# Patch stage of a vision tower: ScalarE writes the normalised rows two units ahead

## The reference

```python
x = features.reshape(B, c, h, 16, w, 16) -> (B, h * w, 16 * 16 * 3)   # 196 patches of 768 numbers an image
x = _layernorm(x, ln1_g, ln1_b)                                       # over the 768
x = jnp.einsum('bnd,de->bne', x, W) + b                               # to 192 features
x = _layernorm(x, ln2_g, ln2_b)                                       # over the 192
h = x                                                                 # the tokens; attention and the rest follow
```

## Time and profile before

| | us |
|---|---|
| time of the kernel, median of three runs | 3089.83 (3086.55 to 3103.68) |
| the profiled execution: its own time | 3087.19 |
| the profiled execution: span of the instructions | 3085.5 |
| patch stage in it: first `xn` to last `yn` | 31.6 to 368.0 |
| busy over the whole span: PE, PEld, DVE, ACT, POOL | 2732.0, 2124.6, 2311.9, 1878.1, 1682.0 |

### The profile page before, as it was taken

The page is one execution under the profiler, slowest core; times in us unless marked ns, Lnnn a source line. Parts: engine busy times, 40 slices in busy tenths (PEclk is TensorE's granted clock), DMA queues, the critical chain, the costliest instruction groups (busy, mean ns, idle before and its releaser), DMA issues. The chain is left out here.

```text
span 3085.5 us, 95504 instructions
## 1 busy us (share of the span) xinstructions
PE 2732.0 (89%) x31491; PEld 2124.6 (69%) x31491; DVE 2311.9 (75%) x5326; ACT 1878.1 (61%) x3798; POOL 1682.0 (55%) x1957
## 2 busy tenths in 40 slices
PE   5798788999899998989998967999986999999998
PEld 5688645555555555555555546899975888888887
DVE  5689678788878887877788735877765777777776
ACT  5577556667666666666666636777753444444443
POOL 3467635555455666667666432567674444444444
PEclk9899989999999999999999968999987999999999
DMA  6555256676766667676767635444433444444443
GB/s 159 161 157 166 58 121 155 145 164 149 157 142 152 165 163 167 161 173 160 175 159 174 143 76 136 147 147 147 143 126 91 68 67 65 68 67 65 69 66 47
DMA packets 515433, 395.07 MB, mean 128 GB/s; under 512 B 223136, under 2 KB 488386, under 8 KB 515138
## 3 DMA queue, kind: packets, MB, share of 16 engines
q1 hardware_dynamic: 431426, 310.47, 41.3%
q0 software_dynamic: 38496, 46.38, 8.5%
q10 hardware_dynamic: 45216, 34.34, 4.6%
HBM read 232.59 MB, written 155.42 MB: 126 GB/s over the span
## 5 line engine op out<-in xcount | busy, mean ns | idle before, releaser
L814 DVE TENSOR_REDUCE a_mx<-a_mxp 98x4 f32<-98x784 f32 x768 | 747.0, 973 | 268.6 <-PE a_mxp L1000 265.9
L603 ACT ACTIVATE a_pt<-a_st 98x784 f32<-98x784 f32 x768 | 634.6, 826 | 352.8 <-PE a_st L986 351.9
L1817 POOL DMA_INDIRECT out_dram<-f_yo,f_idg x202 | 330.9, 1638 | 415.6 <-DVE f_yo L2158 378.9
L500 POOL TENSOR_TENSOR a_cf<-a_ctxs,a_rec 128x1176 f32<-128x1176 f32 x64 | 171.6, 2681 | 448.1 <-DMA a_rec<-a_recip 448.1
L1895 ACT ACTIVATE f_hf<-f_bank,f_b1c 128x256 f32<-128x256 f32 x606 | 254.3, 473 | 236.0 <-PE f_bank L1128 236.0
L1015 PE MATMUL a_pv<-a_pt,a_vp 98*32 98x196 f32 x6144 | 358.7, 352 | 5.0 <-issue 4.1
L986 PE MATMUL a_st<-a_qst,a_kst 49*128 49x196 f16 x3072 | 266.7, 253 | 78.6 <-DMA a_qst<-a_mrow 53.5
L2320 PE MATMUL f_bank<-f_w2h,f_hh 128*128 x1212 | 298.9, 247 | 19.0 <-DVE f_hl L2142 18.7
L2321 PE MATMUL f_bank<-f_w2h,f_hl 128*128 x1212 | 298.2, 246 | 0.0
L2322 PE MATMUL f_bank<-f_w2l,f_hh 128*128 x1212 | 298.2, 246 | 0.0
L1000 PE MATMUL a_mxp<-a_kst,a_qst 48*128 48x196 f16 x3072 | 263.6, 250 | 28.8 <-DVE a_mx L814 21.5
(11 more groups left out here) (314 smaller groups left out, 8269.9 us busy)
## 6 DMA issues: line engine op xcount, KB each, us to landing
a_rec<-a_recip SPq DMA_DIRECT2D x256, 147.0 KB, 4.9
t_rows<-in_x_dram SPq DMA_DIRECT2D x84, 392.0 KB, 5.7
a_qst<-a_qk SPq DMA_DIRECT2D x256, 110.2 KB, 3.2
a_kst<-a_qk SPq DMA_DIRECT2D x256, 110.2 KB, 4.0
f_xg<-f_listed SPq DMA_DIRECT2D x101, 264.0 KB, 2.8
a_qk<-a_qkh SPq DMA_DIRECT2D x128, 196.0 KB, 3.1
a_qk<-a_qkl SPq DMA_DIRECT2D x128, 98.0 KB, 3.4
a_qk<-a_qkh SPq DMA_DIRECT2D x128, 98.0 KB, 2.5
```

What stands on the lines that cost most here:

```text
L603: act.activation(pt[k % PT][:].rearrange("p j a t -> p j (a t)"), st_ps[0:half_t, :, 0:unit_t], ACT.Exp, scale=sm_scale).then_inc(exp_s, 1)
L814: dve.tensor_reduce(mx[:, a, :, 2 * p:2 * p + 2].rearrange("p q j -> p j q"), mx_ps[0:half_t, :, 0:unit_t].rearrange("p j (q t) -> p j q t ...
L1817: pool.indirect_dma_start(out, bass.IndirectOffsetOnAxis(ap=idg[i % 3][:, t:t + 1], axis=0), yo[i % 3][:, t, :], None, compute_op=ALU.add) ...
```

## The change

In ScalarE's step the instructions change places. Before they were rows of unit s + 1, high parts of unit s + 1, results of unit s - 1. They become high parts of unit s + 1, rows of unit s + 2, results of unit s - 1. The rows' own waits move with them (written for the unit they belong to), and the rows of unit 0 are done ahead of the first high parts. Nothing else is touched: same instructions, same buffers, the other four streams as they were.

```diff
             def step(s, kinds):
                 if "B" in kinds:
                     u, b = s + 1, (s + 1) % 2
-                    g, v = divmod(u, UPG)
-                    gb = g % 2
-                    for t in range(2):
-                        wait(act, norm_s, NORM * (u + 1))
-                        wait(act, tr_s, 2 * (u - 1) + t + 1)
-                        act.activation(xn[t][:].rearrange("r (a x) -> r a x", x=patch), patches(rows[gb], 2 * v + t), ACT.Identity,
-                                       scale=rstd[u % 3][:, t:t + 1], bias=shift[u % 3][:, t:t + 1]).then_inc(xn_s, 1)
+                    if u == 0:
+                        normed_rows(0)
                     for t in range(2):
                         wait(act, tr_s, 2 * u + t + 1)
                         wait(act, yp_s, u - 1)
                         act.copy(xh[b][t][:].rearrange("p (a k) r -> p a (k r)", a=2), turned[t][:, :, 0:KT // 2 * R]).then_inc(xh_s, 1)
+                    if u + 1 < NU:
+                        normed_rows(u + 1)
 
                 if "D" in kinds:
                     normalise(s - 1, (s - 1) % 2)
+
+            def normed_rows(u):
+                g, v = divmod(u, UPG)
+                for t in range(2):
+                    wait(act, norm_s, NORM * (u + 1))
+                    wait(act, tr_s, 2 * (u - 1) + t + 1)
+                    act.activation(xn[t][:].rearrange("r (a x) -> r a x", x=patch), patches(rows[g % 2], 2 * v + t), ACT.Identity,
+                                   scale=rstd[u % 3][:, t:t + 1], bias=shift[u % 3][:, t:t + 1]).then_inc(xn_s, 1)
```

## The result

| | before | after |
|---|---|---|
| time, median of four runs beside each other, us | 3092.7 (3086.55 to 3103.68) | 3144.39 (3136.37 to 3151.2) |
| ratio after to before | | 1.0166, 95% interval 1.0127 to 1.0205 |
| the profiled execution: time, span | 3087.19, 3085.5 | 3151.2, 3149.5 |
| 42 steps, results of unit 11 to those of unit 53 | 233.59 | 281.96 |

A forecast was written before the change was run, and what follows sets the result against it. It took a ring of ACT's results and POOL's gain, bias and norms to bound the patch stage, lengthened from 4.95 to 6.85 us. Terms 1.9 + 5.2 + 2.7 + 51.9 - 2 gave +59.7, so 3149 us, range 3138 to 3172.

The forecast's parts named there:

- 2, units 0 to 3: Patch stage, results of units 0 to 3: three steps of 6.85 us, 20.55 against 15.33, +5.2 us.
- The mechanism: Patch stage: rows and results wait for the same norms; the move puts 1.90 us of rows between norms and results.
- the signs that the prediction named: Patch stage: steps of 6.8 to 6.9 us, POOL released by ACT, store stall gone, last results near 430.
- Term 1: Results of unit 0: first norms end as before, rows of unit 3 go first, +1.9 us.
- Term 4: Units 11 to 53: 42 steps of 6.85 us, less 2.2 in the last, 285.5 against 233.59, +51.9 us.
- first rival: Patch stage: other stalls of 0.61 us a step stay on top, 25.6 us more, 3175; chance 0.11.
- the ring: Patch stage loop of ACT's results, POOL's gain and bias, POOL's norms: 4.95 us a step before, 6.85 after.
- Other stalls vanish: Patch stage: the 0.61 us a step on top of the ring was expected to disappear.
- Term 3: Units 3 to 11: SP sets the time, store stall melts, group 2 wait stays; rows 1.90 plus 0.8 restart, +2.7 us.
- Term 6: Into the attention: with DVE ahead of the ring, borders are done by the last results' end; -2 us.
- The rule on the clock: Patch stage: PE idling about 1.9 us a step might start each step at the low clock; weighed low.
- the rival of 3192: Patch stage: PE turns cold for good, 0.85 us more over some 50 steps, 42 us, 3192; chance 0.05.

The follow-up runs named there:

- half dose: Changed kernel with only the first of the two row instructions ahead of the results, the second behind: 3109.21 us, ratio 1.0058 to the kernel before.
- copy in two places: Useless ACT copy each step: ahead of the results on the kernel before, ratio 1.0094; behind the results on the changed kernel, ratio 1.0195.
- cut ring: POOL's norms put ahead of gain and bias: 3093.35 us, ratio 1.001 on the changed kernel; 3097.0 us, ratio 1.0035 on the kernel before.
- reduction on DVE: Useless reduction at the end of each DVE step: ratio 1.0056 on the kernel before, 1.0187 on the changed kernel.
- late loads: Second attention layer's weight loads issued at step 10 instead of 5: ratio 0.9945 on the kernel before, 1.0153 on the changed kernel.
- the first group: Runs on one chip: half dose, copy ahead of the results, both kernels with the cut ring, and the kernel before at 3088 us.

## Why the prediction was right

Forecast 3149 us, measured 3144.4. The nearness of the two flatters the sum: it forecast a loss of 59.7 us, and against the four runs of before the loss is 51.7. Each term of the sum against its measured value, the ends read from the starts of results above:

| term | forecast | measured | how |
|---|---|---|---|
| start of the stage | 0 | -1.44 | first rows at 30.12, before 31.56: the start's own variation |
| 1, results of unit 0 | +1.9 | +0.86 | 16.29 from the first rows, before 15.43 |
| 2, units 0 to 3 | +5.2 | +4.9 | 20.23 against 15.33 |
| 3, units 3 to 11 | +2.7 | +1.4 | 63.17 against 61.80 |
| 4, units 11 to 53 | +51.9 | +48.4 | 281.96 against 233.59 |
| 5, units 53 to 55 | 0 | -0.3 | 9.14 against 9.41 |
| 6, into the attention | -2 | -0.65 | 2.55 from last results to PE's start, before 3.20 |
| sum | +59.7 | +53.1 | PE's first attention matmul, 423.46 against 370.32 |

**The mechanism** held at each step: same wait for both, rows between norms and results, gain and bias and norms behind them. The half dose, the copy in two places and the cut ring each show a part of it. Of the signs that the prediction named, these came: POOL is released by ACT in every step, it never waits for DVE's product statistics between 135 and 400 us, and the stall on the store is gone. The step is 6.74 where 6.8 to 6.9 was written, and the last results came at 420.91 and not near 430.

**Term 1**: the rows are paid in full, 46.41 - 44.55 = 1.86 us from their start to the results. But the norms ahead of them came 1.0 us sooner after the first rows than in before. The likely reason is PE: here it issued 24 matmuls in the 2 us from 38 us on, 7.9 us after the first rows; in before it was at 13 in that slice and at 25 only from 42 us on, 10.4 us after the first rows. That would be a difference of two starts and not of the two orders.

**Term 4** carries the sum, and its miss is the length of the step. I used 4.95 as a ring where the clean one was 4.91 or 4.92, and 1.90 for the rows where ACT gives them up to the next instruction after 1.86. The results behind rows take 0.89, not 0.91. That is 0.09 to 0.10 of the 0.11 between 6.74 and 6.85, and 42 x 0.11 = 4.6 us. Against it two steps are longer than the others (7.06 and 7.38), 1.0 us in all. In the one of 7.38 (unit 18) the gain took 1.63 us instead of 1.00 beside DVE's beside work: what the first rival feared of POOL's slow operations on the ring is real, and small. The last step is 4.56, 2.18 less than the rest: forecast 2.2.

**Other stalls vanish**: right. 38 of the 42 steps lie between 6.73 and 6.76. This is the difference to the rival of 3175, in which 0.61 a step stays. But what I took them for, "something else on top of the ring", was loose. The table of the cut ring shows that the mean of 5.56 was no sum of ring and stalls. It was a mix of steps set by the ring (4.91 to 4.99) and steps set by others: DVE with its beside work (units 14, 16, 29, 36), POOL's beside work (42, 43, 47, 48), PE once (unit 25, 8.19, where ACT waited 3.70 us for the transposes). To take for each step the larger of its old length and the clean one is a good estimate where only the ring is lengthened: for the 41 steps from unit 11 to unit 52 it gives 278.0 us for the changed kernel, measured 277.4, and 246.8 for the half dose, measured 247.5. Where the dose also lengthens another way it falls short: 241.6 against 250.9 with the copy ahead of the results, 238.1 against 248.1 with the reduction on DVE. For this forecast both give the same number, as 6.74 is above nearly all of the others. For the experiments they don't: my expectation for the cut ring and for the reduction on DVE rested on the loose reading, and both were half wrong.

**Term 3**: the stall of 11.6 us on the store is gone and the way from unit 3 to 9 is 40.44 us, six rounds of 6.74. DVE's wait for group 2 went from 22.05 to 15.3, as the ring had come later to it:

```profile
DVE t_stats L1394 <- DMA t_rows<-in_x_dram: 15.3, 1, 15.3
```

From DVE's start on group 2 to the results of unit 11 it is 8.74 us against 6.88, the rows' 1.86 again. So the 0.8 us that I added for PE's restart at the low clock did not show, and the way to group 2 was 0.5 us shorter; that is the 1.3 by which the term was too large. That SP's queue would cover the stretch was right, and the late loads confirm it from the other side: without the cover the change costs 53.96 - 40.72 = 13.2 us there.

**Term 6** was wrong in its reason. DVE should have been ahead of the ring and have had the borders ready. But the borders stand behind DVE's product statistics of unit 55. These waited 3.57 us for PE's matmuls of that unit, and the matmuls had waited 1.26 us for the results of unit 53 (`yp` has two buffers). So DVE can't run far ahead of the ring, and the last border is set at 423.4, just ahead of PE's start; 0.65 came of 2.

**The rule on the clock.** The granted clock did fall in some of the steps. Stretches of 2 us of the changed kernel, columns as in rows 1:

```profile
154.00:156.00 2.00, 0.71 (x9) 0.52 (x7) 1.86 (x8) 0.75 (x1) 1.05 (x3) 1.00 0.30 88
...
158.00:160.00 2.00, 1.90 (x13) 1.89 (x13) 1.87 (x7) 1.66 (x4) 1.85 (x2) 0.50 1.04 285
160.00:162.00 2.00, 2.00 (x18) 2.00 (x17) 0.81 (x2) 0.01 (x1) 1.72 (x5) 0.66 0.38 110
```

From 158 us PE works at 0.50, its lower level of 1.2 GHz, after 0.71 us of work in the slice to 156 and 1.55 in the next. The step does not get longer for it:

```profile
155.25 1.03 ACT L1353 ACTIVATE t_xn<-t_rows,t_shift,t_rstd 112x768 f32<-112x768 f32 x1 [2.77 <-POOL t_shift L1311]
...
161.99 1.03 ACT L1353 ACTIVATE t_xn<-t_rows,t_shift,t_rstd 112x768 f32<-112x768 f32 x1 [2.33 <-POOL t_shift L1311]
...
168.73 1.03 ACT L1353 ACTIVATE t_xn<-t_rows,t_shift,t_rstd 112x768 f32<-112x768 f32 x1 [2.77 <-POOL t_shift L1311]
```

6.74 and 6.74 again. The mean over the stretch is 0.95 against 0.99 before. PE's busy time grew by 19 us (225.76 against 207.07 in 42 steps) and none of it reached the ring. The Trainium skill (TensorE: Matmul & The Clock Gate, "HAM oscillation — how this bites in real kernels") warns that bursts of matmuls with gaps between them begin at the low clock. The trace agrees for single steps, not for all of them, and the rival of 3192 did not come.

Which steps fall is not a matter of the program alone. In the first execution of the changed kernel the falls lie between 144 and 257 us (mean 0.88) and the clock is 1.00 from there to 411; in the second it is 1.00 from 128 to 237 and falls between 237 and 350 (mean 0.86). The clean steps take 6.72 to 6.76 us in all of them. The cost of one cold step was set too high in the prediction as well: by its own figures it is 7.7 - 5.0 = 2.7 us and not 3 to 4.

**What stays open**: why the clock falls in one stretch of steps and not in another, and whether the new order of ACT is worth its 4.9 us once the ring is cut, since the times don't tell 3093 from 3097.

## What to carry to other kernels

Where no engine is full, look for two engines that wait for each other in turn, and write down what stands between the wait and the instruction that the other one needs. Work placed there is charged in full at every step (1.86 us of rows made a clean step 1.83 longer) and work behind it is free (0.82 us of copy made nothing), though the engine is the same and is idle for 39% of the stretch.

A mean step may be a mix of steps with different bounds. Take the shortest ones for the length of the ring, and expect from a cut of the ring only the way to the next bound, in the steps that the ring sets: here 0.3 us in the clean steps, which later stores and late rows took back. And a length from one event to the next hides a bound that moves both of them: look at what released each end.

An operation should be put early in its stream for the one who waits for it last, not for the one who would merely like it sooner: rows came 0.81 us earlier and were of no use. PE did wait for them (21 times, 17.1 us in all from 120 to 360 us in the kernel before), but PE was not what the step waited for.

## What the runs showed of the hardware

- TensorE's clock may fall in single steps of a regular pattern and not in the others, and in other steps in the next execution of the same program: the mean was 0.95 in both, with slices of 0.50 and 1.00 side by side.
- The kernel before took 3088 us on one chip and 3142 on two others, a difference as large as that of the change. It lies in one stage: from SP's first load of the experts' weights to the last write of the output it is 1208 to 1221 us in the traces of before, after and the first group, and 1253 to 1264 in those of the other two groups, while the attention takes 1465 to 1486 in all of them. Only runs of the same group can be compared.
- Two activations of 112 x 192 take 0.89 us behind other work of ACT and 0.91 after a wait.
- A small operation on POOL can be held up by a long one on DVE: of the norms' first operation (0.20 us), seven in the 42 steps of the kernel before took 0.27 to 1.07 us, and each ended 0.06 us after an operation of DVE's beside work did.
